# Attention with group statistics: the low part of GpSimd's two split tiles is made by two DMAs in place of a subtraction

## The reference, cut to what matters

```python
x_f = einsum('oc,bcn->bon', Wf, xf) + bf      # 16 channels
x_g = einsum('oc,bcn->bon', Wg, xf) + bg      # 16 channels
x_h = einsum('oc,bcn->bon', Wh, xf) + bh      # 128 channels
s = einsum('bci,bcj->bij', x_f, x_g)          # 1024 x 1024 per image
beta = softmax(s, axis=-1)
o = einsum('bci,bij->bcj', x_h, beta)
x = x + gamma[0] * o
...
x_n = x_flat / maximum(norm(x_flat, axis=2), 1e-12)
cos = einsum('bcn,bdn->cd', x_n, x_n) / B
_, idx = top_k(-abs(cos).T, 4)
# mean and variance over a channel and its partners, then scale and shift
```

## Time and profile before

| | |
|---|---|
| median of 2 runs | 213.44 us (213.17 to 213.71) |
| the profiled execution | 213.46 us, its span 211.7 us |
| PE busy | 184.7 us, 87% of the span |
| DVE busy | 162.3 us, 77% |
| ACT busy | 133.5 us, 63% |
| POOL busy | 109.1 us, 52% |
| mean granted TensorE clock | 0.944 |

### The profile page before, as it was taken

How to read it: one execution, slowest core, us unless ns; L and a number is a source line. 1 busy time by engine, 2 the same in 40 slices (tenths; PEclk the granted TensorE clock), 3 DMA queues, 4 the chain that set the end, 5 groups by cost and what they waited for, 6 DMA issues and landing times.

```text
span 211.7 us, 2461 instructions
## 1 busy us (share of the span) xinstructions
PE 184.7 (87%) x759; PEld 122.7 (58%) x759; DVE 162.3 (77%) x283; ACT 133.5 (63%) x231; POOL 109.1 (52%) x106
## 2 busy tenths in 40 slices
PE   7949999999999999999999999999999999872000
PEld 3614567667766776577757775777576756541000
DVE  1594889799788988898889888988898886366640
ACT  2267484689648964896589757985698478240420
POOL 4007519922993199419940995099608971910400
PEclk9975999999999999999999999999999999998555
DMA  5300050013000400050005000200020000000297
GB/s 200 159 0 0 0 152 0 0 28 124 0 3 12 136 0 0 0 152 0 2 2 152 0 0 2 50 0 0 3 50 0 0 5 0 0 0 0 104 401 290
DMA packets 4013, 10.71 MB, mean 51 GB/s; under 512 B 544, under 2 KB 672, under 8 KB 4000
## 3 DMA queue, kind: packets, MB, share of 16 engines
q1 hardware_dynamic: 3424, 9.18, 13.4%
q10 hardware_dynamic: 576, 1.38, 1.8%
HBM read 4.52 MB, written 4.19 MB: 41 GB/s over the span
## 4 chain that ended last, share of the span: by engine, by line
PE 74%; DVE 11%; POOL 4%; ACT 3%; issue 3%; DVEq 0%; ACTq 0%; POOLq 0%
PE o_ps L654 41%; PE s_ps L633 13%; PE w_ps L606 6%; PE w_ps L615 6%; DVE nmax L408 3%; PE w_ps L676 3%; PE w_ps L671 3%; PE o_ps L590 2%; ACT probs L329 1%; DVE x_all L583 1%; POOL probs_low L271 1%; DVE fg_parts L425 1%; POOL probs_high L269 1%; DVE probs_low L417 1%; DVE g_low L432 1%
## 5 line engine op out<-in xcount | busy, mean ns | idle before, releaser
L329 ACT ACTIVATE probs<-s_ps,nmax 128x1024 f32<-128x1024 f32 x64 | 71.4, 1115 | 39.4 <-DVE nmax L408 39.4
L408 DVE TENSOR_REDUCE nmax<-s_ps 128x1 f32<-128x1024 f32 x64 | 77.9, 1219 | 12.1 <-PE s_ps L633 12.1
L266 POOL TENSOR_SCALAR probs<-probs,rinv 128x1024 f32<-128x1024 f32 x16 | 24.3, 1522 | 74.2 <-DVE rinv L412 73.5
L654 PE MATMUL o_ps<-probs,vnorm 128*128 128x512 f32 x128 | 60.8, 598 | 0.4 <-DVE x_all L448 0.4
L633 PE MATMUL s_ps<-g_low,fg_parts 128*128 128x512 f32 x128 | 50.6, 478 | 4.1 <-ACT probs L329 3.4
L271 POOL TENSOR_TENSOR probs_low<-probs,probs_high 128x1024 fp32r<-128x1024 f32 x16 | 38.1, 2382 | 1.4
L654 PEld LDWEIGHTS o_ps<-probs,vnorm 128*128 128x128 f32 x128 | 24.5, 192 | 22.8 <-issue 19.2
L633 PEld LDWEIGHTS s_ps<-g_low,fg_parts 128*128 128x128 f32 x128 | 21.2, 194 | 15.2 <-issue 7.7
L654 PE MATMUL o_ps<-probs_high,v_high 128*128 128x512 f32 x64 | 25.3, 396 | 0.8 <-POOL probs_low L271 0.8
L654 PE MATMUL o_ps<-probs_high,v_low 128*128 128x512 f32 x64 | 25.2, 394 | 0.0
L654 PE MATMUL o_ps<-probs_low,v_high 128*128 128x512 f32 x64 | 25.0, 391 | 0.0
(11 more groups left out here) (88 smaller groups left out, 200.8 us busy)
## 6 DMA issues: line engine op xcount, KB each, us to landing
x_all<-x_dram SPq DMA_DIRECT2D x7, 512.0 KB, 3.5
out_dram<-x_all SPq DMA_DIRECT2D x5, 512.0 KB, 6.6
g_low<-fg_parts SPq DMA_DIRECT2D x14, 128.0 KB, 2.2
out_dram<-x_all ACTq DMA_DIRECT2D x2, 512.0 KB, 4.9
x_all<-x_dram SPq DMA_DIRECT2D x2, 256.0 KB, 3.8
out_dram<-x_all SPq DMA_DIRECT2D x2, 256.0 KB, 2.2
wd<-wide_dram ACTq DMA_DIRECT2D x1, 256.0 KB, 4.7
wd<-wide_dram ACTq DMA_DIRECT2D x1, 66.5 KB, 3.4
```

Of the source, the lines that this page charges most:

```text
L266: nc.gpsimd.tensor_scalar(probs[t][:, :], probs[t][:, :], rinv[:, t:t + 1], 1.0, ALU.mult, ALU.mult).then_inc(pool_scaled, 1)
L329: nc.scalar.activation(probs[t][:, :], s_ps[t % 2][:, :], ACT.Exp, bias=nmax[:, t:t + 1], accum_out=rsum[:, t:t + 1]).then_inc(exp_done, 1)
L408: nc.vector.reduce_max(nmax[:, t:t + 1], s_ps[t % 2][:, :], AX_X, negate=True).then_inc(max_ready, 1)
L654: last = nc.tensor.matmul(o_ps[:, halves[h]], weights, rows[:, halves[h]], start=(t == 0 and n == 0), stop=(t == T - 1 and n == len(produc ...
```

## The change

In `split_probs` GpSimd scales the tile as before and SP then issues a DMA that copies the scaled tile (128 x 1024 float32, 512 KB, within SBUF) into probs_low. GpSimd multiplies the scaled tile by -1 into a new float32r buffer `minus_high`, which rounds it, so that it holds minus the high part. Then it makes the high part by the cast as before. It waits for the copy to land (`low_copied`) and for minus_high, and issues a second DMA that adds minus_high to probs_low. TensorE waits for this second DMA (`pool_low`, which now counts in sixteens) and for the cast (`pool_high`). There is one minus_high, so its next writing waits until the DMA that reads it has landed.

```diff
+        minus_high = sb("minus_high", [P, N], F32R)
...
             load(1)
             load(2)
+
+            def copy_low(b, t):
+                sp.wait_ge(pool_scaled, pool_split_count(b, t))
+                sp.dma_start(probs_low[SPLIT.index(t)][:, :].bitcast(F32), probs[t][:, :]).then_inc(low_copied, 16)
+
             for b in range(1, B):
+                for t in POOL_SPLIT:
+                    if t >= TH:
+                        continue
+                    copy_low(b - 1, t)
 
                 for h in range(H):
...
                 if b + 2 < B:
                     load(b + 2)
+                for t in POOL_SPLIT:
+                    if t >= TH:
+                        copy_low(b - 1, t)
+            for t in POOL_SPLIT:
+                copy_low(B - 1, t)
...
                 pool.wait_ge(pool_scaled, count)
+                if count > 1:
+                    pool.wait_ge(pool_low, 16 * (count - 1))
+                nc.gpsimd.tensor_scalar(minus_high[:, :], probs[t][:, :], -1.0, None, ALU.mult).then_inc(minus_ready, 1)
                 nc.gpsimd.tensor_copy(probs_high[n][:, :], probs[t][:, :]).then_inc(pool_high, 1)
-                pool.wait_ge(pool_high, count)
-                nc.gpsimd.tensor_tensor(probs_low[n][:, :], probs[t][:, :], probs_high[n][:, :].bitcast(F32),
-                                        ALU.subtract).then_inc(pool_low, 1)
+                pool.wait_ge(low_copied, 16 * count)
+                pool.wait_ge(minus_ready, count)
+                pool.dma_start(probs_low[n][:, :].bitcast(F32), minus_high[:, :].bitcast(F32),
+                               accum_op=ALU.add).then_inc(pool_low, 16)
...
                     if t in POOL_SPLIT:
-                        pe.wait_ge(pool_low, pool_split_count(b, t))
+                        pe.wait_ge(pool_high, pool_split_count(b, t))
+                        pe.wait_ge(pool_low, 16 * pool_split_count(b, t))
```

More of the change, by code:

```diff
@@ L140, in build @@
         pool_low = sem("pool_low")
+        minus_ready = sem("minus_ready")
+        low_copied = sem("low_copied")
         vn_ready = sem("vn_ready")
```

## The result

| | before | changed |
|---|---|---|
| median of 2 runs | 213.44 us | 257.25 us (256.73 to 257.76) |
| profiled execution, its span | 213.46, 211.7 | 256.73, 254.9 |
| mean granted TensorE clock | 0.944 | 0.892 |

The changed kernel takes 1.203 times as long, with a 95% interval of 1.196 to 1.210. The forecast was 258 us with a range of 236 to 288. The medians and ranges of the experiments are over all their runs, and the ratios leave out four slow ones, over 1.5% longer than the fastest of their kernel (one each in experiments one, six, seven and twelve).

The account below looks back on a forecast made before the run. TensorE was taken to bound the kernel, with GpSimd's low parts costing only when late. Seven images at 3.75 + 1.7 (38.2), first tile 2.1 and last tile 4.1 give 44.4 on 213.5: 258 us, range 236 to 288.

Parts of the forecast that it names:

- The bound and the margins: Steady images: TensorE always busy, so low parts cost only when late; margins 1.36 us at tile 7, 1.27 at tile 2.
- Scaled to landed: From scaled tile to low part: copy 3.5 us, then accumulating DMA 5.2; multiplication (1.1) and cast hidden beside the copy.
- Tile 7 stalls: Images 0 to 6: low part lands at 84.0, TensorE wants it at 80.26, a stall of 3.75 us each.
- Tile 2 nearly hides: Next image's tile 2 lands at 92.6, wanted at 92.0 after tile 7's stall: 0.6 us, swallowed if the clock falls.
- The clock: TensorE's clock falls to 0.50 after most tile 7 stalls; price 0 to 3.4 us, middle 1.7 taken per image.
- First tile: Tile 2 of image 0: low part lands at 26.9 where TensorE came at 24.80, costing 2.1 us.
- Last tile: Tile 7 of image 7: low part lands at 188.8, TensorE now starts at 184.71, already 0.80 late; costs 4.1 us.
- Hidden at no cost: SP's queue, g copies behind tile 2's copy, and DVE and ACT work priced at nothing; minus_high's rewriting no loss.
- Rival 1: Accumulation as cheap as a load and clock up: 235 us; with 5.2 and clock up, 250. Chance 0.28 (232 to 251).
- Rival 2: Accumulation costs 8.7 us, so the single minus_high makes tile 2 late too: 298 us. Chance 0.18 (272 to 300).
- Rival 3: DVE's L417 holds up GpSimd's DMA writing, 1.3 us for each of 16, at most 20: up to 279 us. Chance 0.05.
- rival 4: Each DMA takes little more than a fixed 2.2 us, both tiles come in time: 213 us. Chance 0.04.

Follow-up runs that it names:

- experiment one: Changed kernel with the multiplication by -1 written with two scalar operations (times -1, times 1): 246.3 us, ratio 1.153.
- experiment six: Changed kernel plus two DVE float32 copies of 128 x 1024 between spare buffers once tile 7's cast is done, images 0 to 6: 258.93 us, ratio 1.213.
- experiment seven: Changed kernel, but only tile 7 is made by the two DMAs and tile 2 keeps the subtraction: 253.08 us, ratio 1.182.
- twelve: Changed kernel with two-operation multiplication, both DMAs in halves, and TensorE waiting for the low part only before the low products: 235.2 us, ratio 1.100.
- eight: Changed kernel, but only tile 2 is made by the two DMAs and tile 7 keeps the subtraction: 254.88 us, ratio 1.192.
- experiment five: Changed kernel with the subtraction back, no multiplication by -1, and copies and accumulations sent to a spare buffer: 224.64 us, ratio 1.054.
- two: Changed kernel without SP's copy into probs_low and the waits for it: 256.19 us, ratio 1.203.
- experiment three: Changed kernel with GpSimd's second DMA copying minus_high over probs_low instead of adding it: 241.37 us, ratio 1.132.
- experiment four: Changed kernel with twelve filling matmuls on zeros before TensorE's wait at tile 7, images 0 to 6: 254.36 us, ratio 1.194.

## Why the prediction was right, point by point

The forecast was 258 us and the measured time is 257.25. That the two are so close is luck: with the multiplication at its forecast price the kernel takes 246.3 us (experiment one), 12 below the forecast and still in the range. The dear multiplication made up for terms that were set too high. The mechanism was right: a chain longer than its margin, one stall per image at tile 7, tile 2 in its shadow.

| start of TensorE's work on | before | changed | later by | predicted |
|---|---|---|---|---|
| tile 2, image 0 | 24.80 | 27.01 | 2.2 | 2.1 |
| tile 7, image 2 | 80.26 | 96.19 | 15.9 | 2.1 + 2 x 5.45 + 3.75 = 16.75 |
| tile 7, image 7 | 184.71 | 227.24 | 42.5 | 44.4 |

- **The bound and the margins.** Right. A low part costs time once its chain passes the margin; experiments seven and eight show it for each tile by itself. But the margins are not all: in experiment five both low parts are in time in the steady images, and 11.4 us are lost.
- **Scaled to landed, 3.5 + 5.2 = 8.7.** The sum was right (87.45 to 96.19), its parts were not. The step that failed is "a multiplication by -1 (taken at 1.1 ...)", with "lies beside SP's copy and costs nothing". The multiplication takes 2.8 us, with the cast 3.8, longer than the copy's 2.9. So GpSimd's own work took the copy's place on the path (0.3 more than the 3.5), and the accumulation was 0.3 to 0.6 shorter than 5.2. Experiments one and two show both sides: with the multiplication at 1.15 the copy is what is waited for, and with it at 2.88 the copy can go and nothing changes.
- **The accumulation.** The estimate was a load plus one more read of 512 KB, 1.7 us. The add costs 1.6 us (experiment three), the base is 3.0 and not 3.5.
- **Tile 7 stalls, 3.75 us.** 3.2 to 3.4 in the steady images, 3.96 in image 0.
- **Tile 2 nearly hides, 0.6 us.** Right: nothing in five of the six images where the clock had fallen, 0.93 us where it hadn't, and the two costs alone are nearly twice the cost of the pair. The exception is image 7, 0.98 us behind a fall; with the clock kept up it waits 2.62 there (experiment four).
- **The clock, 1.7 us at each stall.** The fall lasts 3.4 us and costs 1.7. The forecast's 1.7 was the middle between no fall and one of 6.8 us as in the earlier trace rows, so that the figures agree is luck. In experiment seven a fall adds 1.6 us to TensorE's busy time in an image. But beside tile 2's wait the net price is smaller. Windows with and without a fall differ by 0.3 to 0.7 us (26.44 and 26.89 against 26.16), and keeping the clock up gained 0.4 for each stall (experiment four). The prediction said that the fall swallows the 0.6 of tile 2; it swallows 0.93. An image costs 4.6 to 5.3 us more where 5.45 was said.
- **First tile.** 2.2 against 2.1, where only 0.84 is idle time. The rest is a clock that stood at 0.50 for longer while the pipeline filled, from about 12.2 to 22.5, where it had been from 13.7 to 20.5. It fell before GpSimd scaled its first tile at 17.15, so that fall is no effect of the change, and that the sums agree is luck:

```profile
10.00:13.00 3.00, 0.91 (x4) 0.47 (x3) 2.82 (x5) 1.64 (x3) 0.00 (x0) 0.87 0.00 0
...
22.00:23.00 1.00, 1.00 (x4) 0.43 (x4) 0.00 (x0) 0.00 (x0) 1.00 (x3) 0.76 0.00 0
```

- **Last tile.** It waited 5.60 where it had waited 0.80: 4.8 against 4.1. Its multiplication took 3.62 us, and its first 1.0 us lay beside DVE's operation on tile 6 (L439, L417 before), the one that held the scaling in the earlier trace rows. Tile 7 of image 0 has the same pair, and 3.62 too:

```profile
217.49 1.43 DVE L439 SCALAR_TENSOR_TENSOR probs_low<-probs,rinv,probs_high 128x1024 fp32r<-128x1024 f32 x1 [0.87 <-ACT probs_high L360]
...
217.93 3.62 POOL L289 TENSOR_SCALAR minus_high<-probs 128x1024 fp32r<-128x1024 f32 x1
...
227.24 0.76 PE L677 MATMUL o_ps<-probs_high,v_high 128*128 128x512 f32 x1 [5.60 <-DMA probs_low<-minus_high]
```

- **Hidden at no cost.** Right for SP's queue and for minus_high (one wait of 0.4 us). Right for the g copies in this kernel, for the reason given, and experiments five and eight show what they cost where that reason is gone.
- **The rivals.** Rival 1's price with the accumulation at its estimate and the clock up, 250, is not what came: with the clock up it is 254. Rival 2's dear accumulation and rival 4's free one are excluded by 4.6. Rival 3's 16 holds of 1.3 us are 20.8 and not "at most 20", and its hold has no occasion in the changed kernel: none of the 16 issues lies beside an L439 (L417 before), and they take 0.89 to 1.08 us. Experiment six tried copies in its place, which start after the issue, and one issue of seven grew by 0.3 us.

Open is why a multiplication with one operation is dear on GpSimd, what lengthens the smaller waits of experiment five, and what a DVE operation does to an issue that comes after it.

## What to carry to other kernels

Before you replace an instruction by transfers, take the distance from input ready to result wanted and put the whole new chain against it, the issue and the fixed part of every DMA included: here 4.95 us were there, and a copy and an accumulation, one after the other, need 7.5 (2.9 + 4.6) at the least. Price a new instruction by a row of the same form, not only of the same size. Where two late results follow each other, the first stall pays for most of the second, so mending one of them alone gives back little.

## What the runs showed of the hardware that was not expected

- On GpSimd a multiplication of 128 x 1024 float32 into float32r takes 2.88 us with one operation and 1.15 with two (experiment one).
- A DMA that adds takes 4.6 us for 512 KB within SBUF and 3.6 for 256 KB (two of them 0.9 us apart), against 3.0 (GpSimd) or 2.9 (SP) for a plain copy of 512 KB. Its issue holds GpSimd for 0.92 us, a plain one's for 0.62 (experiment three).
- Two DVE copies that start 0.1 us after the issue change neither its 0.90 us nor the median landing of 4.6; in one image of seven, where they start 0.32 us after it, the issue takes 1.23 (experiment six).
- Beside DVE's L439, which reads two tensors in SBUF, GpSimd's multiplication takes 3.62 us in place of 2.77 (images 0 and 7 of the changed kernel).
- Small copies that run beside accumulations land in 3.6 us in place of 2.2, and loads from HBM behind them in 4.4 in place of 3.5 (experiment five; 3.7 and 4.3 in experiment eight).
